# First projection and first feed-forward product of an audio tower: five passes of 128 rows in place of six of 96

## The chip, the core and the metric

The kernel runs on one core of one Trainium2 chip. The metric is device microseconds (us) of one execution, lower is better. Most numbers below are microseconds from the start of the profiled span; the granted clock of TensorE is given as a share of its full speed, 1.00 for 2.4 GHz and 0.50 for 1.2 GHz.

## The reference: what is computed

Eight batches of 750 frames with 192 channels go through three blocks, each ending in 375 tokens of 192 channels. The second and third block are added to a running sum.

```
tok:  depthwise convolution (7 taps) -> pointwise 192x192 -> relu -> max over pairs of frames
      -> real part of a 2-d DFT -> layer norm
attn: n = layernorm(h);  w = n @ w_qkv            (192 -> 768)   <- the first projection
      w is normed over tokens per head; its squares and temp give a softmax over the tokens;
      weighted squares give a gate per head and channel;  -(w * Pi) * gate @ w_out + b_out
ffn:  z = layernorm(h); normed = ln(z); sigmoid scores; the 56 lowest tokens get self-attention,
      the others a mix with a pooled row;  h = z + merged
      n2 = ln(h, g2, b2);  h + gelu(n2 @ W1 + bf1) @ W2 + bf2    <- W1 (192 -> 768): the first
                                                                    feed-forward product
```

## The kernel before

All data of one batch is on the chip: tokens stand either on 125 partitions times three tiles, or, turned, with channels on partitions and the tokens along the free dimension. A software pipeline of three stages runs over the batches: in one step the **front** stage works on batch p (convolution, DFT, first projection, token softmax), the **middle** stage on batch p-1 (routing, keys, attention) and the **last** stage on batch p-2 (feed-forward). Every engine has its own program, written out by hand in `step` (one for each engine), and semaphores join them. So the order on each engine is fixed by the text: an instruction that waits holds up all that stand behind it on that engine. Steps 2 to 7 have all three stages; step 0 has only the front, step 1 no last stage, step 8 no front, step 9 only the last stage.

Products that need more precision than one pass of the type fp32r gives are done in parts. The operand is split into a high part (a ScalarE copy that rounds to fp32r) and a low part (a VectorE subtraction), and high by high, high by low and low by high are summed in PSUM. `split_product` (line 1087) issues these three matmuls, at line 1090. 192 channels are two tiles of 96 partitions (C = 96, CT = 2), so one output tile of 128 channels by 376 tokens takes six matmuls, each with its own weight load: three for each half of the channels.

The two products that the change touches:

- The **first projection**, `qkv(b, j)` on TensorE (line 1138), j = 0 to 5. It comes behind `front_input` (line 1132), six transposes that turn the normed tokens into the PSUM tensor xb; ScalarE copies the high parts (line 892) and VectorE subtracts the low parts (line 468). The result goes to one of two PSUM banks; ScalarE's `squares` copies and squares it (lines 901 and 902), and `qkv(b, j)` waits for the squares of j-2. On ScalarE the squares are interleaved with the middle stage's exponentials (line 977) and with copies of the turned probabilities (line 982). When the last square is done, VectorE makes `rhead` (line 480), for which TensorE's `token_logits` (line 1156) waits.
- The **first feed-forward product**, `forward_up(b, j)` (line 1330), j = 0 to 5, behind `forward_input` (line 1326, also six transposes, into zb). Here one ScalarE copy (line 998) and one VectorE subtraction (line 703) serve both channel halves. The six groups are spread between other work: the first ahead of the middle stage's transposes (`routed_input`), the second ahead of `score_sums` (line 1210), the third and fourth behind the rank sums, the fifth and sixth between small products. ScalarE's `gelus` (line 1004) empty the two banks.

The weights of both are loaded once, with channels on 96 partitions, into a scratch view (`w_qkv32`, laid over the tile probsT), and split there: ScalarE makes the high part (line 869), VectorE the low part (line 408). The W1 load is issued by the sync engine's queue after w_qkv's low part is done.

Of the kernel before, what the change touches and what calls it, by code (L numbers as in the profile page):

```python
# [5 lines left out]
N = S // 2  # L6
P, T = 125, 3
C, CT = 96, 2
H1, IT = 12, 6
# [3 lines left out]
NE = N + 1  # L13
# [21 lines left out]
def audio_tower(nc, dram, out):  # L35
    fp32, bf16, fp32r = mybir.dt.float32, mybir.dt.bfloat16, mybir.dt.float32r
    ALU, ACT, AX = mybir.AluOpType, mybir.ActivationFunctionType, mybir.AxisListType

    with ExitStack() as ctx:
        def sb(name, shape, dt=fp32):  # L40
            return ctx.enter_context(nc.sbuf_tensor(name, shape, dt))

        def signal(name, per_batch=1):
            return Signal(ctx.enter_context(nc.semaphore(name)), per_batch)
# [8 lines left out]
        rows = sb("rows_sb", [P, 8, D])  # L53
        w_qkv = sb("w_qkv_sb", [C, 2, CT, IT * 128], fp32r)
        temp = sb("temp_sb", [128, IT])
# [16 lines left out]
        slot = sb("slot_sb", [Q, 1])  # L72
        w_1 = sb("w_1_sb", [C, 2, CT, IT * 128], fp32r)
        b_1 = sb("b_1_sb", [128, IT])
# [8 lines left out]
        zed = sb("zed", [P, T, D])  # L83
        n2T = sb("n2T", [C, 2, CT, NE], fp32r)

# [8 lines left out]
        xh = even  # L94
        xhT = sb("xhT", [C, 2, CT, NE], fp32r)

# [54 lines left out]
        att = sb("att", [Q, D])  # L151
        w_qkv32 = probsT[0:C].rearrange("c j t q -> c (j t q)")[:, 0:CT * IT * 128].rearrange("c (t i) -> c t i", t=CT)
        w_1_32 = w_qkv32
        n2 = sb("n2", [P, T, D])
# [4 lines left out]

        gelu = sb("gelu", [128, IT, NE])  # L160
        res_f = sb("res_f", [P, T, D])
        y_out = res_f
# [57 lines left out]
        n2t_done, n2_done = signal("n2t_done", T), signal("n2_done", T)  # L220
        n2T_ready, n2T_high, n2T_done = signal("n2T_ready"), signal("n2T_high"), signal("n2T_done")
        w1_ready, gelu_done = signal("w1_ready", IT), signal("gelu_done", IT)
# [4 lines left out]
        def tok(t):  # L227
            return slice(P * t, P * (t + 1))
# [35 lines left out]
        def split_parts(k):  # L264

            weight, parts = ((w_qkv32, w_qkv), (w_1_32, w_1), (w_k32, w_k), (w_v32, w_v), (w_m[:], w_mp))[k]
            return weight, parts[:, 0, :, 0:weight.shape[-1]], parts[:, 1, :, 0:weight.shape[-1]]
# [77 lines left out]
        def _(dve):  # L345
# [110 lines left out]
            def second_norm(b):  # L456
# [3 lines left out]
                for t in range(T):  # L460
                    dve.tensor_scalar(xh[:, t, :], res[:, t, :], ln2[1][:, t, 0:1], ln2[3][:, t:t + 1],
                                      ALU.subtract, ALU.mult).then_inc(xh_done.sem, 1)

            def front_input(b):

                for c in range(CT):
                    dve.wait_ge(*xhT_high.of(b, c + 1))
                    dve.tensor_tensor(xhT[:, 1, c, 0:N], xb[0:C, c, 0:N], xhT[:, 0, c, 0:N], ALU.subtract).then_inc(xhT_done.sem, 1)  # L468

# [230 lines left out]
            def forward_input(b):  # L700

                dve.wait_ge(*n2T_high.of(b))
                dve.tensor_tensor(n2T[:, 1, :, 0:N], zb[0:C, 0:2, 0:N], n2T[:, 0, :, 0:N], ALU.subtract).then_inc(n2T_done.sem, 1)  # L703

# [96 lines left out]
        def _(pool):  # L801
            pool.memset(half3[:], -0.5).then_inc(consts.sem, 1)
            for tokens in (xhT, n2T, nT):
                pool.memset(tokens[:, :, :, N:NE].bitcast(fp32), 0.0).then_inc(pads.sem, 1)
            pool.memset(w_v[:, :, :, D + 1:DV].bitcast(fp32), 0.0).then_inc(pads.sem, 1)
# [52 lines left out]
        def _(act):  # L858
# [26 lines left out]
            def front_input(b):  # L885
                act.wait_ge(*xhT_ready.of(b))
                if first(b):
                    act.wait_ge(pads.sem, PADS)
                else:
                    act.wait_ge(*qkv_ready.before(b))  # L890
                for c in range(CT):
                    act.activation(xhT[:, 0, c, 0:N], xb[0:C, c, 0:N], ACT.Copy).then_inc(xhT_high.sem, 1)
                if first(b):
                    act.wait_ge(consts.sem, FILLS)
# [97 lines left out]
            def forward_input(b):  # L992
                act.wait_ge(*n2T_ready.of(b))
                if first(b):
                    act.wait_ge(pads.sem, PADS)
                else:
                    act.wait_ge(*w1_ready.before(b))
                act.activation(n2T[:, 0, :, 0:N], zb[0:C, 0:2, 0:N], ACT.Copy).then_inc(n2T_high.sem, 1)  # L998

# [76 lines left out]
        def _(pe):  # L1076
            mm = pe.matmul

            def transposes(src, dst):
                for c in range(CT):  # L1080
                    for t in range(T):
                        ins = pe.transpose(dst[0:C, c, tok(t)], src[:, t, chan(c)], ident[0:P, 0:P])  # L1082
                return ins

            pe.wait_ge(first_in.sem, FIRST)

            def split_product(o, a, b, start, stop):

                for k, l in ((0, 0), (0, 1), (1, 0)):
                    ins = mm(o, a[:, k], b[:, l], start=start and k + l == 0, stop=stop and k == 1)  # L1090
                return ins

            def pointwise(b, q):
# [38 lines left out]
            def front_input(b):  # L1132
                if first(b):
                    pe.wait_ge(norm_in.sem, NORM)
                pe.wait_ge(*xh_done.of(b))
                transposes(xh, xb).then_inc(xhT_ready.sem, 1)

            def qkv(b, j):

                if j == 0:  # L1140
                    if first(b):
                        pe.wait_ge(pads.sem, PADS)
                        pe.wait_ge(lows.sem, 1)
                if j >= 2:
                    pe.wait_ge(*sq_done.of(b, j - 1))
                for c in range(CT):
                    if j == 0:
                        pe.wait_ge(*xhT_done.of(b, c + 1))
                    ins = split_product(xb[:, j % 2, 0:NE], w_qkv[:, :, c, 128 * j:128 * j + 128], xhT[:, :, c, :], c == 0, c == 1)
                ins.then_inc(qkv_ready.sem, 1)  # L1150
# [175 lines left out]
            def forward_input(b):  # L1326
                pe.wait_ge(*n2_done.of(b))
                transposes(n2, zb).then_inc(n2T_ready.sem, 1)

            def forward_up(b, j):  # L1330
                if j == 0:
                    pe.wait_ge(*n2T_done.of(b))
                    if first(b):
                        pe.wait_ge(lows.sem, WEIGHTS)
                        pe.wait_ge(*prob_done.of(b))
                    else:
                        pe.wait_ge(*y_done.before(b))
                if j >= 2:
                    pe.wait_ge(*gelu_done.of(b, j - 1))
                for c in range(CT):  # L1340
                    ins = split_product(yb[:, j % 2, 0:NE], w_1[:, :, c, 128 * j:128 * j + 128], n2T[:, :, c, :], c == 0, c == 1)
                ins.then_inc(w1_ready.sem, 1)
# [207 lines left out]
```

## Time and profile before

| what | us |
|---|---|
| runs of the kernel | 609.90, 615.81, 616.28; median 615.81 |
| the profiled execution | 609.72 |
| its span, first to last instruction | 607.8 |
| TensorE matmuls busy | 536.7 (88% of the span) |
| VectorE busy | 427.9 (70%) |
| ScalarE busy | 234.5 (39%) |
| GpSimd busy | 68.5 (11%) |
| mean granted clock of TensorE | 0.927 |

The span is 1.9 us shorter than the profiled execution's own time. That execution is one of the lower ones: it stands 1% under the median. Busy time of TensorE counts each matmul with its run through the array, in which the next one already streams; the pace of a row of matmuls is read from the chain of waits or from the start of one group to the start of the next, not from the mean duration. The busy shares are means over ten steps with different limits.

### The profile page before, as it was taken

To read this page: it belongs to the slowest core of one execution; us is meant where nothing else is said; L and a number is where in the kernel's file an instruction comes from. 1 tells how busy PE (TensorE), PEld (TensorE's weight loads), DVE (VectorE), ACT (ScalarE), POOL (GpSimd) and SP (SyncE) were. 2 spreads that over 40 slices of the span, in tenths; PEclk is the share of its full clock that TensorE was granted. 3 is DMA by queue.
4 is the path that set the end of the run, shared out by engine and by line. 5 is a ranking of instruction groups with operands and counts; after the bars stand their busy time and mean duration, and the time that the engine had idled before them with its cause. 6 is when DMAs were issued, how large, how long until landed. Compare 5 with 4: busy or idle time off the path is not lost.

```text
span 607.8 us, 9498 instructions
## 1 busy us (share of the span) xinstructions
PE 536.7 (88%) x3344; PEld 444.4 (73%) x3344; DVE 427.9 (70%) x1239; ACT 234.5 (39%) x619; POOL 68.5 (11%) x67
## 2 busy tenths in 40 slices
PE   1637498979999999999999999999999999969896
PEld 1426286758877888778887987797778877856586
DVE  6777658675778987798878887887788473843240
ACT  1134113530458135811582257315651457014611
POOL 0010001100030003001210121011200120001000
PEclk9986589676999999999999999999999999967698
DMA  9531000010000100010001000100000000000000
GB/s 215 145 73 38 1 2 1 0 39 1 1 1 5 36 20 1 1 40 19 0 0 38 19 0 0 38 19 0 0 0 20 1 1 1 6 15 1 1 9 30
DMA packets 8217, 12.73 MB, mean 21 GB/s; under 512 B 1896, under 2 KB 6722, under 8 KB 8189
## 3 DMA queue, kind: packets, MB, share of 16 engines
q1 hardware_dynamic: 8189, 12.37, 7.7%
q8 instruction: 16, 0.26, 0.2%
q14 instruction: 12, 0.10, 0.0%
HBM read 10.07 MB, written 2.30 MB: 20 GB/s over the span
## 4 chain that ended last, share of the span: by engine, by line
PE 59%; DVE 16%; ACT 13%; issue 9%; POOL 1%; DMA 1%; ACTq 0%; DVEq 0%; SPq 0%; POOLq 0%
PE xb L1175 9%; PE yb L1090 8%; PE zb L1090 7%; PE xb L1120 5%; ACT w_sq L902 3%; ACT probs L977 3%; PE xb L1129 3%; ACT w_s L901 2%; DVE dw L401 2%; PE xb L1090 2%; DVE w_sq L508 2%; DVE junk L516 2%; PE xb L1156 2%; PE zb L1322 2%; PE yb L1352 2%
## 5 line engine op out<-in xcount | busy, mean ns | idle before, releaser
L815 POOL TENSOR_TENSOR rs<-ve,half 125x3 f32<-125x3 f32 (+1 forms) x32 | 33.4, 1045 | 407.3 <-DVE ve L366 329.6
L383 DVE SCALAR_TENSOR_TENSOR dw<-x_in,w_dw_sb,dw 96x750 f32<-96x750 f32 x84 | 79.0, 990 | 0.2
L1090 PE MATMUL xb<-xhT,w_qkv_sb 96*128 96x376 f32 x288 | 63.6, 366 | 4.8 <-DVE xhT L468 3.4
L1090 PE MATMUL yb<-n2T,w_sb 96*128 96x376 f32 x288 | 60.6, 352 | 4.2 <-DVE n2T L703 3.2
L1090 PEld LDWEIGHTS xb<-xhT,w_qkv_sb 96*128 96x128 f32 x288 | 52.4, 204 | 11.3 <-DVE xhT L468 6.8
L1175 PE MATMUL xb<-scratch,w_sq 128*125 128x192 f32 x288 | 53.0, 347 | 4.1 <-ACT scratch L913 4.1
L1175 PEld LDWEIGHTS xb<-scratch,w_sq 128*125 128x125 f32 x288 | 51.6, 203 | 4.9 <-DVE scratch L530 4.5
L1090 PEld LDWEIGHTS yb<-n2T,w_sb 96*128 96x128 f32 x288 | 49.3, 192 | 6.9 <-DVE n2T L703 4.2
L1352 PE MATMUL yb<-w_sb,gelu 128*125 128x192 f32 x252 | 47.5, 331 | 0.0
L1352 PEld LDWEIGHTS yb<-w_sb,gelu 128*125 128x125 f32 x252 | 40.7, 187 | 2.8 <-issue 2.8
L1120 PE MATMUL xb<-dft_n_sb,pooled_h 125*96 125x376 f32 x96 | 34.2, 510 | 1.0 <-DVE pooled_h L417 0.9
L982 ACT ACTIVATE probsT<-zb 125x384 f32<-125x384 f32 x48 | 26.4, 551 | 21.2 <-PE zb L1286 21.2
L913 ACT ACTIVATE scratch<-w_out_sb,natt 128x192 f32<-128x192 f32 x24 | 9.2, 445 | 64.9 <-DVE natt L528 64.9
L1286 PEld LDWEIGHTS zb<-ident_sb,probs 128*125 128x125 f32 x144 | 23.0, 207 | 13.5 <-issue 10.5
L1004 ACT ACTIVATE gelu<-yb,b_sb 128x375 f32<-128x375 f32 x48 | 26.7, 570 | 14.1 <-PE yb L1090 12.7
L1110 PE MATMUL xb<-w_pw_sb,dw 97*125 97x192 f32 x64 | 17.9, 364 | 14.7 <-DVE dw L401 14.2
L998 ACT ACTIVATE n2T<-zb 96x750 fp32r<-96x750 f32 x8 | 6.3, 792 | 62.1 <-PE zb L1082 62.1
L1286 PE MATMUL zb<-ident_sb,probs 128*125 128x128 f32 x144 | 28.3, 311 | 2.0 <-ACT probs L977 2.0
L508 DVE TENSOR_TENSOR w_sq<-w_s,xb 128x376 f32<-128x376 f32 x48 | 25.2, 538 | 4.8 <-PE xb L1167 4.8
L901 ACT ACTIVATE w_s<-xb 128x375 f32<-128x375 f32 x48 | 25.4, 530 | 6.3 <-PE xb L1090 6.2
L1120 PEld LDWEIGHTS xb<-dft_n_sb,pooled_h 125*96 125x96 f32 x96 | 16.1, 174 | 15.4 <-issue 15.1
L902 ACT ACTIVATE w_sq<-xb 128x375 f32<-128x375 f32 x48 | 25.8, 537 | 0.0
(190 smaller groups left out, 1104.5 us busy)
## 6 DMA issues: line engine op xcount, KB each, us to landing
x_in<-in_x SPq DMA_DIRECT2D x8, 567.0 KB, 4.2
out<-res_f SPq DMA_DIRECT2D x7, 281.2 KB
probsT<-in_w_qkv SPq DMA_DIRECT2D x1, 576.0 KB, 7.5
w_out_sb<-in_w_out SPq DMA_DIRECT2D x1, 576.0 KB
w_sb<-in_w SPq DMA_DIRECT2D x1, 576.0 KB
probsT<-in_w SPq DMA_DIRECT2D x1, 576.0 KB, 4.2
rows_sb<-in_rows SPq DMA_DIRECT2D x1, 504.0 KB
dft_n_sb<-in_dft_n SPq DMA_DIRECT2D x1, 493.5 KB
```

The source lines that it names most:

```text
L383: ins = dve.scalar_tensor_tensor(out=dw[0:C, c, :], in0=src, scalar=w_dw[:, c, k:k + 1], in1=dw[0:C, c, :], op0=ALU.mult, op1=ALU.add)
L508: dve.tensor_tensor(u[:, j, :], w_s[:, j, :], xb[:, j % 2, 0:NE], ALU.mult).then_inc(u_done.sem, 1)
L815: pool.tensor_tensor(out_[:], in_[:], half3[:] if len(in_.shape) == 3 else half3[:, 0, :], ALU.pow).then_inc(rs.sem, 1)
L901: act.activation(w_s[:, j, 0:N], xb[:, j % 2, 0:N], ACT.Copy)
L902: act.activation(w_sq[:, j, 0:N], xb[:, j % 2, 0:N], ACT.Square, accum_out=nrm[:, j:j + 1]).then_inc(sq_done.sem, 1)
L982: act.activation(probsT[:, j, :, :], zb[0:P, 2 + j % 2, 0:T * 128].rearrange("p (t q) -> p t q", q=128), ACT.Copy).then_inc(prT_done.sem, 1)
L1004: act.activation(gelu[:, j, 0:N], yb[:, j % 2, 0:N], ACT.Gelu, bias=b_1[:, j:j + 1]).then_inc(gelu_done.sem, 1)
L1090: ins = mm(o, a[:, k], b[:, l], start=start and k + l == 0, stop=stop and k == 1)
L1120: ins = mm(xb[0:C, c, 0:2 * KF], pooled_h[:, t, chan(c)], dft_n[:, t, :], start=(t == 0), stop=(t == T - 1))
L1175: ins = mm(o, u[:, j, tok(t)], w_oa[:, j, :], start=(j == 0), stop=(j == IT - 1))
L1286: ins = pe.transpose(zb[0:P, 2 + j % 2, 128 * t:128 * t + 128], probs[:, j, tok(t)], ident[:])
L1352: ins = mm(o, gelu[:, j, tok(t)], w_2[:, j, :], start=(j == 0), stop=(j == IT - 1))
```

## The change

The 192 channels are cut 128 + 64 in place of 96 + 96. The tokens' tile gets three slots of 128 partitions: slot 0 is the high part of channels 0 to 127, slot 2 their low part, and slot 1 holds both parts of channels 128 to 191, the low part on partitions 0 to 63 and the high part on partitions 64 to 127. The weights get four slots: 0 and 2 are the high and low part of channels 0 to 127, 1 and 3 those of channels 128 to 191, each written twice, once above the other. So five matmuls with 128 rows give the sum, and it holds low by low for the last 64 channels besides. The transposes take 128 columns each, the second one channels 64 to 191, so that channels 128 to 191 come out on partitions 64 to 127.

The feed-forward tokens are now split by two ScalarE copies and two VectorE subtractions, one pair for each slot, where one of each served before. The two weight loads carry 128 partitions (the last 64 channels twice: 768 KB each in place of 576 KB), and their scratch view lies over the tile gelu in place of probsT. The pad memsets follow the new shape.

```diff
-        w_qkv = sb("w_qkv_sb", [C, 2, CT, IT * 128], fp32r)
+        w_qkv = sb("w_qkv_sb", [128, 4, IT * 128], fp32r)
-        n2T = sb("n2T", [C, 2, CT, NE], fp32r)
+        n2T = sb("n2T", [128, 3, NE], fp32r)
-        xhT = sb("xhT", [C, 2, CT, NE], fp32r)
+        xhT = sb("xhT", [128, 3, NE], fp32r)
...
+        w_qkv32 = gelu[:].rearrange("c j n -> c (j n)")[:, 0:2 * IT * 128].rearrange("c (t i) -> c t i", t=2)
+        w_1_32 = w_qkv32
...  VectorE
+            def stacked_low(c, parts, bank):
+                if c == 0:
+                    return dve.tensor_tensor(parts[:, 2, 0:N], bank[:, 0, 0:N], parts[:, 0, 0:N], ALU.subtract)
+                return dve.tensor_tensor(parts[0:64, 1, 0:N], bank[64:128, 1, 0:N], parts[64:128, 1, 0:N], ALU.subtract)
             def front_input(b):
                 for c in range(CT):
                     dve.wait_ge(*xhT_high.of(b, c + 1))
-                    dve.tensor_tensor(xhT[:, 1, c, 0:N], xb[0:C, c, 0:N], xhT[:, 0, c, 0:N], ALU.subtract).then_inc(xhT_done.sem, 1)
+                    stacked_low(c, xhT, xb).then_inc(xhT_done.sem, 1)
             def forward_input(b):
-                dve.wait_ge(*n2T_high.of(b))
-                dve.tensor_tensor(n2T[:, 1, :, 0:N], zb[0:C, 0:2, 0:N], n2T[:, 0, :, 0:N], ALU.subtract).then_inc(n2T_done.sem, 1)
+                for c in range(CT):
+                    dve.wait_ge(*n2T_high.of(b, c + 1))
+                    stacked_low(c, n2T, zb).then_inc(n2T_done.sem, 1)
...  ScalarE
-                    act.activation(xhT[:, 0, c, 0:N], xb[0:C, c, 0:N], ACT.Copy).then_inc(xhT_high.sem, 1)
+                    act.activation(xhT[64 * c:128, c, 0:N], xb[64 * c:128, c, 0:N], ACT.Copy).then_inc(xhT_high.sem, 1)
-                act.activation(n2T[:, 0, :, 0:N], zb[0:C, 0:2, 0:N], ACT.Copy).then_inc(n2T_high.sem, 1)
+                for c in range(CT):
+                    act.activation(n2T[64 * c:128, c, 0:N], zb[64 * c:128, c, 0:N], ACT.Copy).then_inc(n2T_high.sem, 1)
...  TensorE
+            def stacked_transposes(src, dst):
+                for c in range(CT):
+                    for t in range(T):
+                        ins = pe.transpose(dst[0:128, c, tok(t)], src[:, t, 64 * c:64 * c + 128], ident[0:P, 0:P])
+                return ins
+            def stacked_product(o, w, j, x, rest=None):
+                cols = slice(128 * j, 128 * j + 128)
+                mm(o, w[:, 0, cols], x[:, 0, :], start=True, stop=False)
+                mm(o, w[:, 2, cols], x[:, 0, :], start=False, stop=False)
+                if rest is not None:
+                    pe.wait_ge(*rest)
+                mm(o, w[:, 0, cols], x[:, 2, :], start=False, stop=False)
+                mm(o, w[:, 1, cols], x[:, 1, :], start=False, stop=False)
+                return mm(o, w[:, 3, cols], x[:, 1, :], start=False, stop=True)
             def qkv(b, j):
-                for c in range(CT):
-                    if j == 0:
-                        pe.wait_ge(*xhT_done.of(b, c + 1))
-                    ins = split_product(xb[:, j % 2, 0:NE], w_qkv[:, :, c, 128 * j:128 * j + 128], xhT[:, :, c, :], c == 0, c == 1)
+                if j == 0:
+                    pe.wait_ge(*xhT_done.of(b, 1))
+                ins = stacked_product(xb[:, j % 2, 0:NE], w_qkv, j, xhT, xhT_done.of(b) if j == 0 else None)
             def forward_up(b, j):
-                for c in range(CT):
-                    ins = split_product(yb[:, j % 2, 0:NE], w_1[:, :, c, 128 * j:128 * j + 128], n2T[:, :, c, :], c == 0, c == 1)
+                ins = stacked_product(yb[:, j % 2, 0:NE], w_1, j, n2T)
...  host: the weights' layout
+    def stacked(w):
+        return np.stack([w[0:128], np.concatenate([w[128:], w[128:]])], 1)
```

## Rows read from the trace of the kernel before

**Rows 1.** Stretch, us, busy of PE, PEld, DVE, ACT, POOL; clock, DMA share, GB/s:
```profile
282.93:346.35 63.42, 61.81 (x419) 51.86 (x419) 52.07 (x151) 28.65 (x77) 8.41 (x7) 1.00 0.05 14
```

**Rows 2.** Chain of waits in that step: start, us, what ended last:
```profile
282.93 1.02 PE yb L1090 x6
283.95 0.64 PE zb L1082 x6
...
293.41 0.33 PE zb L1210 x3
...
307.14 0.79 PE xb L1082 x6
...
308.03 0.49 ACT xhT L892
...
320.05 0.47 ACT w_sq L902 x2
```

**Rows 3.** A stretch inside the first projection, columns as in rows 1:
```profile
316.00:318.00 2.00, 2.00 (x15) 2.00 (x14) 2.00 (x4) 2.00 (x9) 0.00 (x0) 1.00 0.00 0
```

**Rows 4.** TensorE in order of time: start, us, instructions, idle before, releaser:
```profile
309.14 2.33 PE L1090 MATMUL xb<-xhT,w_qkv_sb 96*128 96x376 f32 x12 [0.39 <-DVE xhT L468]
...
321.39 1.45 PE L1156 MATMUL xb<-w_sq,rhead 128*32 128x375 f32 x12 [0.60 <-DVE rhead L480]
...
326.38 0.61 PE L1167 MATMUL xb<-pi_parts,head_sel_sb 128*128 128x376 f32 x2 [0.27 <-DVE pi_parts L501]
```

**Rows 5.** One line's matmuls: ns minimum/median/maximum, 128 rows and 96:
```profile
L1167 PE MATMUL xb<-pi_parts,head_sel_sb x48: 332/437/682, 64.8 to 521.2; 128*128 128x376 f32 x48
...
L1090 PE MATMUL xb<-xhT,w_qkv_sb x288: 328/334/682, 48.5 to 508.5; 96*128 96x376 f32 x144
```

**Rows 6.** VectorE, and one group of weight loads (PEld), in order of time:
```profile
281.11 0.93 DVE L703 TENSOR_TENSOR n2T<-zb,n2T 96x750 fp32r<-96x750 f32 x1
281.96 1.07 DVE L557 SCALAR_TENSOR_TENSOR nr<-nr,rs,rows_sb 125x192 f32<-125x192 f32 x3
...
292.82 0.18 DVE L590 RECIPROCAL nr<-sexp 125x3 f32<-125x3 f32 x1
293.09 0.46 PEld L1210 LDWEIGHTS zb<-ident_sb,nr 125*125 125x125 f32 x3
...
305.13 0.96 DVE L461 TENSOR_SCALAR even<-res,ag,rs 125x192 f32<-125x192 f32 x3 [0.38 <-POOL rs L815]
...
308.54 1.00 DVE L468 TENSOR_TENSOR xhT<-xb,xhT 96x375 fp32r<-96x375 f32 x2 [1.68 <-ACT xhT L892]
```

**Rows 7.** TensorE in order of time, steps 0 and 1:
```profile
48.49 9.71 PE L1090 MATMUL xb<-xhT,w_qkv_sb 96*128 96x376 f32 x36 [1.24 <-DVE xhT L468]
...
112.68 4.08 PE L1090 MATMUL xb<-xhT,w_qkv_sb 96*128 96x376 f32 x12
...
126.02 1.97 PE L1156 MATMUL xb<-w_sq,rhead 128*32 128x375 f32 x12 [2.45 <-DVE rhead L480]
```

**Rows 8.** TensorE in order of time, steps 8 and 9:
```profile
535.85 1.80 PE L1090 MATMUL yb<-n2T,w_sb 96*128 96x376 f32 x6 [3.17 <-DVE n2T L703]
...
590.38 3.35 PE L1090 MATMUL yb<-n2T,w_sb 96*128 96x376 f32 x18 [0.54 <-DVE res_f L711]
```

**Rows 9.** Stretches of steps 0 and 1, columns as in rows 1:
```profile
50.00:55.00 5.00, 5.00 (x18) 5.00 (x17) 5.00 (x8) 2.39 (x8) 0.00 (x0) 0.50 0.01 3
...
125.00:130.00 5.00, 3.98 (x33) 2.13 (x36) 3.54 (x8) 1.56 (x6) 0.00 (x0) 0.68 0.21 64
```

**Rows 10.** ScalarE in order of time, start-up:
```profile
25.57 1.47 ACT L869 ACTIVATE w_qkv_sb<-probsT 96x1536 fp32r<-96x1536 f32 x1
...
47.29 0.85 ACT L892 ACTIVATE xhT<-xb 96x375 fp32r<-96x375 f32 x2 [8.30 <-PE xb L1082]
```

**Rows 11.** DMA issues: size, microseconds from issue to landing:
```profile
probsT<-in_w_qkv SPq DMA_DIRECT2D x1, 576.0 KB, 7.5
...
probsT<-in_w SPq DMA_DIRECT2D x1, 576.0 KB, 4.2
```

More of the change, by code:

```diff
@@ L72, in audio_tower @@
         slot = sb("slot_sb", [Q, 1])
-        w_1 = sb("w_1_sb", [C, 2, CT, IT * 128], fp32r)
+        w_1 = sb("w_1_sb", [128, 4, IT * 128], fp32r)
         b_1 = sb("b_1_sb", [128, IT])
@@ L151, in audio_tower @@
         att = sb("att", [Q, D])
-        w_qkv32 = probsT[0:C].rearrange("c j t q -> c (j t q)")[:, 0:CT * IT * 128].rearrange("c (t i) -> c t i", t=CT)
-        w_1_32 = w_qkv32
         n2 = sb("n2", [P, T, D])
@@ L220, in audio_tower @@
         n2t_done, n2_done = signal("n2t_done", T), signal("n2_done", T)
-        n2T_ready, n2T_high, n2T_done = signal("n2T_ready"), signal("n2T_high"), signal("n2T_done")
+        n2T_ready, n2T_high, n2T_done = signal("n2T_ready"), signal("n2T_high", CT), signal("n2T_done", CT)
         w1_ready, gelu_done = signal("w1_ready", IT), signal("gelu_done", IT)
@@ L264, in split_parts @@
         def split_parts(k):
-            weight, parts = ((w_qkv32, w_qkv), (w_1_32, w_1), (w_k32, w_k), (w_v32, w_v), (w_m[:], w_mp))[k]
+            if k < 2:
+                parts = (w_qkv, w_1)[k]
+                return w_qkv32, parts[:, 0:2, :], parts[:, 2:4, :]
+            weight, parts = ((w_k32, w_k), (w_v32, w_v), (w_m[:], w_mp))[k - 2]
             return weight, parts[:, 0, :, 0:weight.shape[-1]], parts[:, 1, :, 0:weight.shape[-1]]
@@ L802, in _ @@
             pool.memset(half3[:], -0.5).then_inc(consts.sem, 1)
-            for tokens in (xhT, n2T, nT):
-                pool.memset(tokens[:, :, :, N:NE].bitcast(fp32), 0.0).then_inc(pads.sem, 1)
+            for tokens in (xhT, n2T):
+                pool.memset(tokens[:, :, N:NE].bitcast(fp32), 0.0).then_inc(pads.sem, 1)
+            pool.memset(nT[:, :, :, N:NE].bitcast(fp32), 0.0).then_inc(pads.sem, 1)
             pool.memset(w_v[:, :, :, D + 1:DV].bitcast(fp32), 0.0).then_inc(pads.sem, 1)
@@ L1135, in front_input @@
                 pe.wait_ge(*xh_done.of(b))
-                transposes(xh, xb).then_inc(xhT_ready.sem, 1)
+                stacked_transposes(xh, xb).then_inc(xhT_ready.sem, 1)
             def qkv(b, j):
@@ L1327, in forward_input @@
                 pe.wait_ge(*n2_done.of(b))
-                transposes(n2, zb).then_inc(n2T_ready.sem, 1)
+                stacked_transposes(n2, zb).then_inc(n2T_ready.sem, 1)
             def forward_up(b, j):
@@ L1514 @@
         "ident": np.eye(128, dtype=f),
-        "w_qkv": tiles(a["L0_attn_w_qkv"], C),
+        "w_qkv": stacked(a["L0_attn_w_qkv"]),
         "temp": a["L0_attn_temp"][:, 0][head],
@@ L1533 @@
         "slot": np.where(q < SEL, q, -1).astype(f)[:, None],
-        "w_1": tiles(a["L0_ffn_W1"], C),
+        "w_1": stacked(a["L0_ffn_W1"]),
         "b_1": a["L0_ffn_bf1"].reshape(IT, 128).T,
```

## The prediction

> **What bounds the kernel now.** I read the table of stretches first. A full step lasts 63.42 us, TensorE is busy in 61.81 of it at a granted clock of 1.00 [rows 1]; steps 2 to 7 are all of this kind. That is only a first hint, since a busy matmul includes its run through the array. So I read the chain of waits inside one such step [rows 2]. It has two parts. From 282.93 to 307.93 it goes through TensorE alone, from group to group, and the six groups of the feed-forward product lie in it. From 308.03 to 320.5 it goes through ScalarE, which is busy without a gap (2.00 of 2.00 us, [rows 3]) with exponentials, squares and copies; the six groups of the first projection lie beside it. Then VectorE makes rhead, and TensorE, which has been idle for 0.60 us, starts the token logits at 321.39 [rows 4]. The rest of the step is softmax, spread and the long output product, which the change does not touch. So the two halves of the change must be priced apart: one shortens TensorE where it ends last, the other where ScalarE does.
>
> **A pass.** In the chain six passes take 1.02 us [rows 2], so one costs 0.17 us at full clock, though a single matmul lasts at least 328 ns [rows 5]: they overlap. The trace has no row of consecutive passes with 128 rows and 376 columns. The nearest is the spread, which has that shape: its shortest matmul lasts 332 ns against 328 for 96 rows [rows 5]. Bounds for what a pass with 128 rows costs more: nothing, and 0.03 us, a fifth, at which five would cost as much as six. I take nothing, as the two minima differ by 1%.
>
> A rule of the Trainium skill speaks about this overlap (TensorE: Matmul & The Clock Gate, Part 3): a weight load runs beside matmuls in flight only if it goes to another row group. By it each pass would pay load and matmul in turn, the removed pass would be worth about twice as much, and the full steps would gain some 10 us more. The trace disagrees: 0.17 us a pass leaves no room for it.
>
> **Transposes.** Twelve per full step get weight loads of 128 columns in place of 96. Six with 96 columns take 0.64 us in the chain, 0.107 each; three with 125 columns take 0.33 us, 0.110 each [rows 2]. So 12 x 0.003 = 0.04 us per step at most; I take zero. The skill has a price for this that speaks against the change (same page, LDWEIGHTS): a load costs its columns divided by 1.2 in ns. By that 32 more columns are 27 ns, an estimate of 0.3 us per step if nothing hid it, and the sum would be 2 to 3 us worse. The rows show that it is hidden.
>
> **Full steps, feed-forward product.** Six passes go, 6 x 0.17 = 1.02 us. What is late next, group by group:
> - First group: behind it the transposes need nr, done at 281.96 + 1.07 = 283.03, and run from 283.95 in the chain [rows 2, 6]. The split of the feed-forward tokens into two pieces puts a second instruction on VectorE just ahead of nr: two such halves of the projection's tokens cost 1.00 us together against 0.93 for the one [rows 6], so nr comes 0.07 us later. That leaves over 0.5 us of slack, and the 0.17 us is won. The second ScalarE copy is off the chain.
> - Second group: score_sums waits for the reciprocal that ends at 292.82 + 0.18 = 293.00, and its weight load starts at 293.09 [rows 6]. Here only about 0.05 us is won, the rest becomes a wait.
> - The other four groups: full, 0.68 us. The next thing that could be late is the transposes of the projection's input, which need xh at 305.13 + 0.96 = 306.09 [rows 6] and start at 307.14 [rows 2]; 1.05 us of slack, and xh itself, which hangs on score_sums by way of VectorE and GpSimd, moves 0.22 us forward with it.
>
> Sum 0.17 + 0.05 + 0.68 = 0.90 us per step, six steps: **5.4 us**. Bounds: 0 and 6.1 us.
>
> **Full steps, first projection.** Six more passes go, but ScalarE has no gap to give up. The first group cannot end sooner, as its last three passes still wait for the second low part, and before, too, three passes followed that wait. So zero; TensorE only comes to the token logits earlier and waits there, about 0.5 us longer on top of 0.60 [rows 4], the rest spread in front of the later groups. It is hidden by ScalarE; if that cover were gone it would be worth up to 1 us per step.
>
> **Steps 0 and 1.** In step 0 there are no exponentials on ScalarE, and TensorE is granted 0.50 until about 55 us [rows 9]. 36 passes take 9.71 us [rows 7], 0.27 each, so six fewer are 1.6 us at most; once the clock is back ScalarE's copy and square come close, so I take 0.95. In step 1 the first two groups take 4.08 us for 12 passes [rows 7], 0.34 each; two passes less are 0.68 before ScalarE rules again; I take 0.6.
>
> **Steps 8 and 9.** In step 8 six passes take 1.80 us when the clock is down [rows 8], 0.30 each: two groups at that price and four at 0.17 are 1.3 us, less 0.1 for the extra split instruction, which lies in the open there: 1.2. In step 9 the first three groups take 3.35 us for 18 passes [rows 8], and gelu and the second product alternate with them; six passes at 0.17 are 1.0. The entry of step 9 waits for the result of the batch before, not for the split, so nothing is lost there.
>
> **Start-up.** Both weight loads grow by a third. At their own time to landing, 7.5 and 4.2 us [rows 11], that is at most 2.5 and 1.4 us. The copy of w_qkv runs at 25.57, long after its load, which is issued within the first 10 us; after the copy of W1 ScalarE idles 8.30 us until the transposes [rows 10]. So zero; without that cover 1.4 us once. The splits themselves cost by their free size, which stays at 1536.
>
> **The sum.** 5.4 + 0.95 + 0.6 + 1.2 + 1.0 = 9.15, say 9.2 us. The profiled execution took 609.72 us (span 607.8 and 1.9 around it): 600.6. Two of the three runs shown lie near 616, and the median of 615.81 is 6 us above the profiled execution; the passes go in either kind of run, so from the median it is 606.6. I predict 606 us.
>
> **Rivals.**
> 1. *The next waits eat half.* If score_sums, the reciprocal or xh are later than the rows suggest, or a pass with 128 rows costs 0.015 us more, the full steps give 2 to 3 us in place of 5.4, and the whole about 6: 610 us from the median. For it: the second group has only 0.09 us of slack. Against: the others have 0.5 or more. Chance 0.15.
> 2. *The clock falls for a short time in each full step.* In step 1 TensorE idled 2.45 us ahead of the token logits [rows 7], and the stretch from 125 to 130 us shows a clock of 0.68 after 1.00 before [rows 9]: 64% of 5 us, 3.2 us, at 1.2 GHz. In full steps the idle there is 0.60 us with the clock at 1.00; the change makes it about 1.1 us and adds small waits before. If the clock fell each time, 3.2 us at half rate would lose 1.6 us of TensorE's work, less the 0.27 us that it waits for the softmax anyway [rows 4]: 1.3 x 6 = 8 us, and 614 us in all, no change. Against: 1.1 us is less than half of the idle time at which it fell. Chance 0.11.
> 3. *Slower: the clock stays down.* Same place, but at 1.2 GHz through the spread and the output product, where TensorE is again dense. To decide against the change it must last long: a stretch T of half clock costs T/2 - 0.27 us, and 0.9 us of gain per step is gone at T = 2.3 us; 1% slower needs about 2.55 us per step more, T = 7.5 us. With 12 us it would be 5.7 us in each of six steps, +34 - 9 = +25, 641 us. Against: in step 1 the first fall was over within 3.2 us. Chance 0.07.
> 4. *ScalarE is not the cover.* If the projection's passes count as well, another 4 to 6 us: 601 us from the median. Against it is ScalarE's gapless stretch [rows 3]. Chance 0.05.
>
> That the change does not do what it says I hold excluded: one of six issued matmuls is gone in each group by the text. The forecast itself gets 0.62.
>
> **The numbers.** The forecast is 600.6 to 606.6, with the kind of run deciding; rival 4 pulls the lower end to 598, rivals 1 and 2 the upper end to 614; beyond lies rival 3 and half of rival 2. About 1%, 6 us, is what a measurement of this kernel can tell from no change. Faster by over 1%: forecast and rival 4, 0.67. Within 1%: rivals 1 and 2, 0.26. Slower: 0.07.
>
> **What would show it.** Right: full steps of about 62.5 us; five-pass groups of 0.85 us in the chain; a wait in front of score_sums of about 0.1 us; an idle time of about 1.1 us ahead of the token logits, and ScalarE still without a gap from the table load to the last square; transposes at 0.11 us. Wrong: passes with 128 rows at 0.20 us; a granted clock under 1.00 in the full steps; ScalarE waiting for the projection; the first projection starting late at 48 us because of the larger loads.

## The result, and the profile of the changed kernel

The changed kernel took 596.53 us (median of four runs, 595.51 to 599.11) against 614.83 for the kernel before on the same chip: a ratio of 0.9722, with a 95% interval of 0.9658 to 0.9787. In two more sets of runs the ratio was 0.9775 (0.9684 to 0.9866) and 0.9802 (0.9746 to 0.9858). The forecast was 606 us with a low end of 598: the direction was right, and the gain was about twice the forecast's 9.2 us in the first set, and 14.2 and 10.6 us in the others.

The mean granted clock differs from one execution of the same kernel to the next, from 0.906 (621.4 us) to 0.930 (609.0 us) in 56 runs of the kernel before on four chips, and the time follows it.

The stretches between two starts of the output product show where the profiled execution (596.45 us, span 594.7) is shorter than that of before. Columns as in [rows 1]; the five stretches are the start-up with step 0, step 1, step 2, five full steps, and the end with steps 8 and 9. The kernel before:
```profile
0.00:73.25 73.25, 34.17 (x121) 25.02 (x121) 52.31 (x131) 16.59 (x39) 4.40 (x14) 0.83 0.38 98
73.25:143.52 70.27, 62.87 (x341) 49.90 (x341) 47.23 (x132) 22.19 (x66) 6.04 (x5) 0.79 0.03 9
143.52:208.86 65.34, 63.87 (x420) 53.77 (x420) 51.92 (x151) 28.64 (x77) 8.43 (x7) 0.97 0.04 10
208.86:526.02 317.16, 309.26 (x2091) 259.35 (x2091) 248.20 (x737) 143.20 (x385) 42.06 (x35) 1.00 0.04 10
526.02:607.80 81.78, 66.52 (x378) 56.40 (x376) 28.29 (x91) 23.91 (x52) 7.59 (x6) 0.81 0.04 11
```
The changed kernel:
```profile
0.00:71.26 71.26, 32.11 (x114) 23.38 (x115) 52.50 (x131) 16.73 (x39) 4.41 (x14) 0.83 0.37 106
71.26:137.57 66.31, 56.96 (x334) 44.97 (x335) 47.09 (x133) 22.25 (x66) 6.04 (x5) 0.86 0.03 9
137.57:202.76 65.19, 63.46 (x406) 52.29 (x407) 52.09 (x151) 28.95 (x78) 8.40 (x7) 0.96 0.04 10
202.76:516.64 313.88, 304.95 (x2033) 249.30 (x2032) 250.30 (x742) 144.78 (x390) 42.04 (x35) 1.00 0.04 11
516.64:594.70 78.06, 61.59 (x365) 51.90 (x364) 28.69 (x93) 24.27 (x54) 7.54 (x6) 0.86 0.04 12
```
Five full steps give 317.16 - 313.88 = 3.28, that is 0.66 us each, less than the forecast 0.90. The two ends give 1.99, 3.96 and 3.72, in all 9.7 us, where the forecast had 3.75; step 1 and the end have a higher granted clock than before (0.86 for 0.79, and 0.86 for 0.81).

Inside a full step, first TensorE in order of time (start, us, instructions, idle before): the five passes of the first feed-forward group, the first pass of the projection, and the token logits.
```profile
275.92 0.47 PE L1116 MATMUL yb<-n2T,w_sb 128*128 128x376 f32 x1
276.23 0.33 PE L1117 MATMUL yb<-n2T,w_sb 128*128 128x376 f32 x1
276.39 0.33 PE L1120 MATMUL yb<-n2T,w_sb 128*128 128x376 f32 x1
276.56 0.33 PE L1121 MATMUL yb<-n2T,w_sb 128*128 128x376 f32 x1
276.73 0.33 PE L1122 MATMUL yb<-n2T,w_sb 128*128 128x376 f32 x1
...
301.67 0.44 PE L1116 MATMUL xb<-xhT,w_qkv_sb 128*128 128x376 f32 x1 [0.40 <-DVE xhT L470]
...
314.06 1.45 PE L1186 MATMUL xb<-w_sq,rhead 128*32 128x375 f32 x12 [0.67 <-DVE rhead L489]
```
The passes start 0.17 us apart, as those of 96 rows did [rows 2], and the shortest still takes 328 ns [rows 5]. Then the chain of waits of the same step, where [rows 2] had its counterpart; "issue" is time in which the engine waited for nothing that the profile shows:
```profile
277.07 0.64 PE zb L1094 x6
277.71 3.93 PE xb L1151 x12
...
286.52 0.39 PE zb L1240 x3
...
299.64 0.80 PE xb L1101 x6
300.55 0.49 ACT xhT L903
301.06 0.55 DVE xhT L470
301.88 0.34 issue
302.23 0.35 DVE w_mp L580
302.61 0.56 DVE nmax L653
```
Transposes with 128 columns cost 0.80 us beside 0.79 with 96 in [rows 2]; score_sums has become 0.06 us longer. Two places were not in the forecast. The transform of the pooled tokens (L1151) takes 3.93 us in the chain, where the kernel before has
```profile
284.59 3.79 PE xb L1120 x12
...
309.57 0.35 DVE w_mp L571
...
309.96 0.56 DVE nmax L644
```
and between xhT and the exponentials the chain runs over VectorE, through w_mp to the attention's maximum nmax. The last two lines show that it did so before the change, too; the forecast had read the chain there only up to ScalarE's copy of xhT.

### The profile page after: what moved, and what is told of

Its sections match the earlier page's. It is cut to its first block, busy times and chain, and to the rows that moved or that the text cites. A ratio compares the mean times of both kernels' runs of the same rounds, so it can differ in the third digit from the quotient of the medians.

```text
span 594.7 us, 9326 instructions
## 1 busy us (share of the span) xinstructions
PE 519.1 (87%) x3248; PEld 421.8 (71%) x3248; DVE 430.7 (72%) x1247; ACT 237.0 (40%) x627; POOL 68.4 (12%) x67
## 4 chain that ended last, share of the span: by engine, by line
PE 57%; DVE 18%; ACT 13%; issue 9%; POOL 1%; DMA 1%; DVEq 0%; ACTq 0%; SPq 0%; POOLq 0%
PE xb L1205 9%; PE zb L1109 7%; PE xb L1151 6%; ACT probs L988 3%; PE xb L1160 3%; ACT w_sq L913 3%; DVE w_sq L517 3%; ACT w_s L912 2%; DVE junk L525 2%; DVE dw L404 2%; PE xb L1186 2%; PE yb L1116 2%; PE yb L1381 2%; PE xb L1141 2%; PE xb L1142 2%
## 5 line engine op out<-in xcount | busy, mean ns | idle before, releaser
L1151 PE MATMUL xb<-dft_n_sb,pooled_h 125*96 125x376 f32 x96 | 34.0, 506 | 1.0 <-DVE pooled_h L420 0.9
L1010 ACT ACTIVATE n2T<-zb 128x375 fp32r<-128x375 f32 (+1 forms) x16 | 7.7, 481 | 62.8 <-PE zb L1101 62.6
L1151 PEld LDWEIGHTS xb<-dft_n_sb,pooled_h 125*96 125x96 f32 x96 | 15.7, 171 | 15.7 <-issue 14.6
L1116 PE MATMUL xb<-xhT,w_qkv_sb 128*128 128x376 f32 x48 | 21.1, 439 | 5.6 <-DVE xhT L470 3.5
L525 DVE CUSTOM_DVE_ANT_0 junk<-w_sq,w_s 128x375 f32<-128x375 f32 x48 | 25.4, 540 | 0.0
L1197 PE MATMUL xb<-pi_parts,head_sel_sb 128*128 128x376 f32 x48 | 18.3, 433 | 7.8 <-DVE pi_parts L510 6.5
L1116 PE MATMUL yb<-n2T,w_sb 128*128 128x376 f32 x48 | 20.2, 422 | 4.3 <-DVE n2T L471 3.4
```

What stands on the lines that cost most here:

```text
L525: dve.tensor_tensor_reduce(out=junk[:, j % 2, 0:N], in0=u[:, j, 0:N], in1=w_s[:, j, 0:N], scale=1.0, scalar=0.0, op0=ALU.mult, op1=ALU.add ...
L1116: mm(o, w[:, 0, cols], x[:, 0, :], start=True, stop=False)
L1151: ins = mm(xb[0:C, c, 0:2 * KF], pooled_h[:, t, chan(c)], dft_n[:, t, :], start=(t == 0), stop=(t == T - 1))
```

## The experiments

The questions: is it the missing pass or the height of the passes that makes the ends shorter, and what takes a third of the forecast gain in the full steps? The table has each kernel's median with its ratio to the kernel before on its own chip, the median granted clock of its runs, the time at 1.2 GHz worked out from it run by run as 2 x (1 - clock) x span (the median), and a full step, the mean of the five between starts of the output product in the profile.

| kernel | passes x rows | us | ratio (95%) | clock | us at 1.2 GHz | full step |
|---|---|---|---|---|---|---|
| before (56 runs) | 6 x 96 | 614.81 | | 0.918 | 100.5 | 63.43 |
| changed (16 runs) | 5 x 128 | 599.58 | 0.972 to 0.980 | 0.933 | 80.1 | 62.78 |
| five96 | 5 x 96 | 602.31 | 0.9787 (0.9735, 0.9838) | 0.921 | 95.5 | 62.51 |
| six128 | 6 x 128 | 608.47 | 0.9856 (0.9805, 0.9907) | 0.935 | 78.8 | 63.62 |
| pad128 | 6 x 128, 32 of them zero | 610.35 | 0.9927 (0.9884, 0.997) | 0.937 | 76.7 | 63.43 |
| only_ffn | 5 x 128, 6 x 96 | 602.90 | 0.9756 (0.9705, 0.9806) | 0.927 | 87.8 | 62.63 |
| only_qkv | 6 x 96, 5 x 128 | 610.42 | 0.9938 (0.9897, 0.998) | 0.924 | 92.6 | 63.56 |
| all_rows | 5 x 128 | 597.54 | 0.9729 (0.9662, 0.9797) | 0.937 | 74.4 | 62.78 |
| max_first | 5 x 128 | 602.34 | 0.9815 (0.9737, 0.9892) | 0.926 | 89.5 | 62.63 |
| max_rows (12 runs) | 5 x 128 | 598.10 | 0.9733 and 0.9773 | 0.932 | 81.0 | 62.44 |

In the rows with two counts the feed-forward product stands first. One run of six128 took 1742.57 us; it is left out of the clock columns. The kernel before differs by chip: it spent 102.2 us at 1.2 GHz (median) beside five96, six128, only_ffn and only_qkv, 103.2 beside pad128 and all_rows, and 88.8 beside max_rows and max_first.

**five96**, the kernel before with one pass taken out of each group. It leaves out the product of the weights' low part with the tokens' high part for channels 96 to 191, in both products.
```diff
-  ins = split_product(o, a, b, c == 0, c == 1)
+  if c == 0:
+      return split_product(o, a, b, True, False)
+  mm(o, a[:, 0], b[:, 0], start=False, stop=False)
+  return mm(o, a[:, 0], b[:, 1], start=False, stop=True)
```


> The kernel before with one of its six passes left out in both products (weight low by token high of channels 96 to 191; that part of the sum is missing). Five passes of 96 rows, one split instruction as before. Theory 'passes': as fast as the changed kernel or 1 to 4 us faster, since VectorE's longer split is not paid: 13 to 21 us below the kernel before, full steps 62.4 to 62.6 us. Rival 'rows': only what the forecast counted, 8 to 10 us below the kernel before, and the clock at either end as in the kernel before.

602.31 us, and full steps of 62.51, 0.92 us below the kernel before: the forecast's 0.90 for the passes holds. The clock changed little (0.911 to 0.925 over its runs), as "rows" has it. The time does not fit "rows": 615.86 on the same chip less 602.31 is 13.55 us, inside the 13 to 21 of "passes" and above the 8 to 10 of "rows". So the missing pass is worth more than the forecast had, without any height; the next part compares the kernels at an equal clock.

**six128**, the changed kernel with a sixth pass in each group, the product of the two low parts for channels 0 to 127.
```diff
   mm(o, w[:, 2, cols], x[:, 0, :], start=False, stop=False)
+  mm(o, w[:, 2, cols], x[:, 2, :], start=False, stop=False)
```


> The new layout with a sixth pass put back: low by low of channels 0 to 127, so six passes of 128 rows where the kernel before has six of 96. Theory 'passes': the gain comes from the count alone, so it is gone and the two split instructions remain as cost: full steps 63.4 to 63.8 us, time 0 to +4 us against the kernel before, within 1%. Rival 'rows': passes of 128 rows keep TensorE's granted clock up, or bring it back sooner, in the steps at either end; then the excess over the forecast (some 8 of 17 us) stays: 6 to 9 us faster than before, with clearly less time at 1.2 GHz.

608.47 us. The full steps are 0.19 us longer than before the change, and yet the kernel is 1.4% faster, since its clock was 0.933 to 0.941, above all 17 runs of the kernel before on the same chip (0.906 to 0.930). Where the clock comes back differs between executions: in the profiled one (608.84 us) the start, step 1 and step 2 are shorter than before, and the end is not:
```profile
523.19:607.00 83.81, 67.34 (x378) 57.93 (x376) 28.69 (x93) 24.29 (x54) 7.55 (x6) 0.82 0.04 11
```

**only_ffn** and **only_qkv**, the change in one product alone; the other has its tiles, split, transposes and six passes as before.
```diff
-  xhT = sb("xhT", [128, 3, NE], fp32r)
+  xhT = sb("xhT", [C, 2, CT, NE], fp32r)              # only_ffn; n2T likewise in only_qkv
```


> Only the feed-forward product in five passes of 128 rows; the first projection as before. Theory 'passes': full steps keep the gain but for the 0.16 us that the projection's split costs, 62.6 us each; steps 8 and 9 gain some 3 us; steps 0 and 1 unchanged: 7 to 9 us faster than before. Rival 'rows': the same in the full steps, and step 1's clock as before, so also some 8 us; this run tells where the gain lies rather than why.

> Only the first projection in five passes of 128 rows; the feed-forward product as before. Forecast of record: full steps gain nothing here, steps 0 and 1 1.6 us. Theory 'passes': full steps 63.4 to 63.6 us, steps 0 and 1 together 1.5 to 3 us shorter: 0 to 3 us faster than before, within 1%. Rival 'rows': steps 0 and 1 together 5 to 7 us shorter because the clock is up for longer: 5 to 8 us faster. Rival 'cover': ScalarE is not the bound there and full steps lose 0.5 us or more each: 4 to 6 us faster.

The feed-forward half gives 0.80 us per full step and the projection's half costs 0.13; together 0.67, and the whole change measures 0.66. So the projection's passes are hidden, as forecast, but its new split is not. In time both gain more than "passes" gave them: only_ffn 13.0 us from the 615.86 before (7 to 9 were expected), only_qkv 5.4 (0 to 3).

**pad128** keeps the kernel before and its six passes, and only makes the four tiles 128 rows high, with zeros in rows 96 to 127.
```diff
-  xhT = sb("xhT", [C, 2, CT, NE], fp32r)              # and w_qkv, n2T, w_1
+  xhT = sb("xhT", [128, 2, CT, NE], fp32r)
+  for tile in (xhT, w_qkv, n2T, w_1,):
+      pool.memset(tile[C:128].bitcast(fp32), 0.0).then_inc(pads.sem, 1)
```


> The kernel before, with the tiles of both operands of the projection and of the first feed-forward product made 128 rows high and rows 96 to 127 set to zero: twelve passes of 128 rows a step at the same column count, the splits and the transposes as before, and 32 rows of each pass that add nothing. Theory 'rows' (the passes' height alone brings TensorE back to 2.4 GHz earlier in the steps at either end; it went from some 102 us at 1.2 GHz with 96 rows to some 79 us with six passes of 128): the same 75 to 85 us at half clock, full steps of 63.4 as before, 607 to 610 us, ratio 0.985 to 0.992. Rival 'data' (it is rows that carry values that do so, zeros do not count): half-clock time stays at 95 to 105 us, 614 to 616 us, ratio 0.997 to 1.003. Rival 'split' (the gain at the ends comes from the new splits and transposes, which begin the product in another order): 614 to 616 us as well, but with the clock of before in every stretch.

610.35 us against 616.98, a little more than "rows" gave it (607 to 610, ratio 0.985 to 0.992); the 76.7 us at 1.2 GHz are inside its 75 to 85. Its runs had a granted clock of 0.930 to 0.941, those of the kernel before on that chip 0.906 to 0.930. Its stretches, which answer to the five of the kernel before above:
```profile
0.00:75.10 75.10, 32.88 (x121) 24.23 (x121) 55.49 (x131) 16.71 (x39) 12.20 (x18) 0.85 0.37 96
75.10:145.37 70.27, 62.72 (x340) 49.65 (x340) 47.28 (x132) 22.22 (x66) 6.04 (x5) 0.79 0.03 9
145.37:210.54 65.17, 63.69 (x420) 53.59 (x420) 51.91 (x151) 28.69 (x77) 8.41 (x7) 0.97 0.04 10
210.54:527.69 317.15, 309.12 (x2092) 259.19 (x2092) 248.14 (x737) 143.44 (x385) 42.03 (x35) 1.00 0.04 10
527.69:606.00 78.31, 62.30 (x377) 53.19 (x376) 28.27 (x91) 23.95 (x52) 7.61 (x6) 0.89 0.04 12
```
The five full steps are the same to 0.01 us, and in this execution so is step 1, at 0.79 as before. The end has the same matmuls with the same columns, a clock of 0.89 for 0.81, and is 3.47 us shorter. The start is 1.85 us longer beside GpSimd's 12.20 us of work for 4.40, which holds the added zero fills (that they cause it is not tested). So the height of the passes alone can bring the clock back, zeros included, and the rivals "data" and "split" fall.

**all_rows**: ScalarE copies all 128 rows in both pieces of a split; rows 0 to 63 of the shared part are then written again by VectorE.
```diff
-  act.activation(xhT[64 * c:128, c, 0:N], xb[64 * c:128, c, 0:N], ACT.Copy)
+  act.activation(xhT[:, c, 0:N], xb[:, c, 0:N], ACT.Copy)          # n2T likewise
```


> The changed kernel, with ScalarE's two copies in each stacked split made over all 128 rows, so that no instruction of ScalarE changes its rows from its neighbour's; rows 0 to 63 of the shared part are written by ScalarE and then again by VectorE, as the order of waits has it already. Theory 'range' (two neighbouring instructions overlap only where their rows are the same: two copies of xhT took 0.85 us with 96 rows each and 0.99 with 128 and 64): the pair returns to 0.84 to 0.88 us, and as ScalarE sets the projection's end, each full step shortens by 0.12 to 0.16 us, to some 62.63; in all 595 to 596 us beside 596.5. Rival 'shape' (the pair is longer as the copies are higher or write another place): 0.96 to 1.0 us and full steps of 62.75 to 62.80, no gain.

The copies overlap again, 0.86 us for the two, and the full step stays at 62.78 all the same. ScalarE in order of time in the changed kernel:
```profile
300.55 0.99 ACT L903 ACTIVATE xhT<-xb 128x375 fp32r<-128x375 f32 x2 [0.55 <-PE xb L1101]
...
303.19 0.57 ACT L988 ACTIVATE probs<-zb,nmax 128x375 f32<-128x375 f32 x1
```
and in this one, then a line of its waits in that step (who waited for whom: us in total, times, longest):
```profile
300.99 0.86 ACT L903 ACTIVATE xhT<-xb 128x375 fp32r<-128x375 f32 x2 [0.55 <-PE xb L1101]
```
```profile
ACT probs L988 <- DVE nmax L653: 0.3, 1, 0.3
```
"range" was right about the pair and wrong about the step: ScalarE now waits 0.3 us for VectorE's nmax, ahead of which stand the lows of xhT and w_mp. That gave the next theory, two paths of about equal length into the first exponential.

**max_rows** and **max_first**: w_mp goes on VectorE behind the second maximum, with all_rows' copies and without.
```diff
-  if middle:
-      pooled_row(q)
   for j in range(IT):
       if middle:
           attention_max(q, j)
+          if j == 1:
+              pooled_row(q)
```


> The kernel with ScalarE's copies over all rows, and on VectorE w_mp (0.35 us, first read some 19 us later by a product of TensorE) moved from ahead of the attention's first maximum nmax to behind its second. Theory 'two paths' (ahead of the projection's first exponential, ScalarE waits for nmax, and nmax stands on VectorE behind the two lows of xhT and w_mp; the changed split made both ScalarE's path and VectorE's path 0.14 us longer, so that mending ScalarE's alone gave nothing): here both are short, the idle time of ScalarE ahead of its first probs goes from 0.3 to under 0.1 us, and each full step shortens by 0.2 to 0.3 us, to 62.48 to 62.58; in all 593.5 to 595.5 us in the better runs. Rival 'other end' (the lows of xhT themselves, through TensorE's projection, or the pooled tokens set the step, not nmax): full steps stay at 62.75 to 62.80.

> The changed kernel with that move of w_mp alone, ScalarE's copies as the change has them (0.99 us for two). Theory 'two paths': ScalarE's own path (two copies, the load of its table, a hint) is now the later one; full steps shorten by 0.08 to 0.15 us, to 62.63 to 62.70, half of what both edits give. Rival 'VectorE alone' (ScalarE's copies never counted): the same 62.48 to 62.58 as with both edits. Rival 'other end': 62.75 to 62.80.

The full steps are 62.44 us (62.48 to 62.58 were expected) and 62.63 (62.63 to 62.70), as "two paths" has it, and both rivals fall. The medians, 597.14 and 602.34 us, hang on the clock at the ends, as the table shows. max_first also has five passes of 128 rows, and yet its 89.5 us at 1.2 GHz (83.6 to 105.6, six runs) lie in the range of the kernel before on its chip, 88.8 (85.0 to 109.7). ScalarE of max_rows in order of time shows the wait gone:
```profile
302.99 0.86 ACT L903 ACTIVATE xhT<-xb 128x375 fp32r<-128x375 f32 x2 [0.55 <-PE xb L1101]
303.87 1.28 ACT L1063 ACT_TABLE_LOAD   x1
305.16 0.20 ACT L1063 ACTIVATE table_hint<-ones 1x1 f32<-1x1 f32 x1
305.27 0.55 ACT L988 ACTIVATE probs<-zb,nmax 128x375 f32<-128x375 f32 x1
```
From the copies to the exponential it takes 305.27 - 302.99 = 2.28 us, where the changed kernel takes 303.19 - 300.55 = 2.64; max_first and the kernel before both take 2.51 (305.36 - 302.85 and 310.54 - 308.03). Six full steps at 62.78 - 62.44 = 0.34 us would be 2.0 us in all. Side by side on one chip, as two runs of their own:

> The kernel with all rows copied and w_mp moved, beside the changed kernel on one chip, to see whether it beats both. Full steps of 62.45 to 62.47 us as in the run before. Theory 'two paths' with the ends as they fall: 1.5 to 2.5 us under the changed kernel's run with the same granted clock, some 594 to 595 us at a clock of 0.941 and some 598 at 0.930.

> The changed kernel as it is, beside it: full steps of 62.75 to 62.80 us, some 596.6 us at a granted clock of 0.941 and 599 to 603 at 0.924 to 0.933.

598.13 us (595.96 to 600.04) against 600.43 (597.66 to 601.03), with full steps of 62.45 and 62.76. The 2.3 us are about what the steps promise, but the runs overlap; that it beats the changed kernel is shown for the steps and likely for the whole. The changed kernel beside all_rows was run as

> The changed kernel as it is, on the same chip as the others of this set. All theories: 595 to 599 us, full steps of 62.75 to 62.80 us, 70 to 76 us at half clock; it is the base for the small difference of the kernel with all rows copied.

It took 602.79 us (596.73 to 608.53), more than expected, with clocks of 0.916 to 0.941; its full steps were 62.78. A difference of 5 us from all_rows, whose steps are the same, lies in the clock at the ends (101.9 us at 1.2 GHz in its longest run, 70.2 in its shortest).

## Why the prediction was too small

**The clock at the ends, the step that failed.** "A pass: I take nothing" was right for the full steps and was carried to the ends, where passes were priced at the clock that the trace of before had there [rows 7, 8, 9]. The clock entered the prediction only as something that could fall (rivals 2 and 3); that it could come back was no case at all. Over the runs of the kernel before, each microsecond more at 1.2 GHz goes with 0.36 us more of its time: a straight line through its 56 runs gives 578.9 + 0.36 t, with t the time at 1.2 GHz. The same line through 16 runs of the changed kernel is 570.9 + 0.36 t, with the same slope. So at an equal clock the change is worth 578.9 - 570.9 = 8.0 us, close to the forecast 9.2, and over all chips the other 0.36 x (100.5 - 80.1) = 7.3 us go with the clock. Side by side on one chip it is less: t falls from 103.2 to 91.3 and from 88.7 to 80.3, worth 4.3 and 3.0 us. In the set that was forecast it is more: the changed kernel has t from 70.2 to 80.0, the clocks of the kernel before are not on record there, and by its line 614.83 us stand for t = 99.8; of the 18.3 us some 10 are then the clock.

That the height of the passes can do this is shown by pad128, which changes nothing else of the passes, and by six128: their t (71.5 to 85.7 and 71.3 to 81.3) lies below almost every run of the kernel before on their chips (85.0 to 116.5). The line holds for six128: 607.3 us at its 78.8, and 6 x 0.19 = 1.1 for its full steps, are 608.4, and 608.11 was measured (the median of its five runs with a clock below 1.00). For pad128 it gives 606.5 and 1.85 for the start, 608.4 where 610.35 was measured; 2 us stay open. Height is not all that decides: max_first's six runs gain nothing clear at the clock, and the changed kernel's own six runs beside pad128 reach from 70.2 to 101.9. What else does stays open.

That 8.0 lies near 9.2 is in part luck. By the same line five96, five passes without the new splits, is worth some 11 us at an equal clock: 5.5 in its full steps and over 5 at the ends, where the forecast had 3.75. (Its profile shows 3.3 at the ends, 1.5 up to the end of step 2 and 1.8 behind the full steps, but with 93.6 us at 1.2 GHz for 88.7.) The new splits then take 1.6 us back in the full steps and, as the difference that is left, some 1.4 at the ends, for which the forecast had 0.1. At an equal clock only_ffn is worth 7.6 us and only_qkv 1.8, as "passes" expected of them.

The Trainium skill (TensorE: Matmul & The Clock Gate, Part 1, "What's actually happening") says that the gate follows how busy TensorE has lately been. The runs agree that it is what TensorE does that moves the clock; they add that matmuls of the same number and columns, but of more rows, can move it too.

**The new splits, a term of the full step that was mis-sized.** "nr comes 0.07 us later ... and the 0.17 us is won" failed, and so did the price of nothing for the split of xhT. The prediction sized both by two halves that start at the same row [rows 6]. The stacked pieces start at different rows. VectorE of the changed kernel in order of time, first a piece from row 0, then one from row 64, then nr from row 0:
```profile
274.40 0.54 DVE L470 TENSOR_TENSOR n2T<-zb,n2T 128x375 fp32r<-128x375 f32 x1
274.97 0.55 DVE L471 TENSOR_TENSOR n2T<-zb,n2T 64x375 fp32r<-64x375 f32 x1
275.55 1.08 DVE L566 SCALAR_TENSOR_TENSOR nr<-nr,rs,rows_sb 125x192 f32<-125x192 f32 x3
276.66 0.62 DVE L420 SCALAR_TENSOR_TENSOR pooled_h<-xb,even 125x192 f32<-125x192 f32 x2
```
None starts before the other has ended: from the first low to nr it is 1.15 us. In [rows 6] nr starts 0.85 us after the one low, which is 0.93 us long. So nr is 0.30 us later in place of 0.07. The pooled tokens behind it were, in the kernel before, at
```profile
282.94 0.61 DVE L417 SCALAR_TENSOR_TENSOR pooled_h<-xb,even 125x192 f32<-125x192 f32 x2
```
which is 1.83 us behind the low at 281.11; now it is 2.26. The slack in front of the transposes holds, and the 0.17 us is won there, but the transform that reads the pooled tokens loses 0.14 of it again (3.93 for 3.79). It takes 3.79 in five96 (old split) and in six128 (new split, but the transposes start a pass later), and 3.92 in only_ffn, which has the new split and five passes. The Trainium skill (VectorE: DVE Perf Modes, "Two Vector instructions with no wait between them") has this as a rule: an instruction whose input or output starts in another group of 32 rows than the last one did in that memory is held until all earlier ones are done. The trace agrees on VectorE, by the rows just shown; the prediction should have used it. No run here changes the rows of a piece on VectorE alone.

The split of xhT costs 0.13 us by only_qkv, and the 2.64 us for 2.51 show where: on VectorE the lows end later and push w_mp and nmax, on ScalarE the two copies take 0.99 for 0.85 us. 0.92 for the passes, less 0.14 and 0.13, is 0.65; 0.66 was measured.

**ScalarE as the cover: right with a gap.** The projection's passes are hidden (only_qkv: no gain, so rival 4 falls), and ScalarE is busy throughout their middle, as in [rows 3]:
```profile
310.00:312.00 2.00, 2.00 (x13) 1.73 (x12) 1.85 (x3) 2.00 (x9) 0.00 (x0) 1.00 0.00 0
```
But the argument went from that stretch to the whole path from 308.03 on, whose first 2.5 us belong to VectorE as much as to ScalarE.

**Right by their sizes:** passes of 128 rows at 0.17 us; transposes; a wait of 0.06 us in front of score_sums; the clock at 1.00 in all full steps, so rivals 2 and 3 fall. Rival 1 had the direction of the full steps, 6 x 0.66 = 4.0 us between its 2 to 3 and the forecast's 5.4, but by the new splits and not by the waits that it named. **Wrong by its size, without weight:** the idle time ahead of the token logits went from 0.60 to 0.67 us, not to 1.1. Two sums do not come out: in rival 3 the 2.55 us per step already hold the 0.9, so T is 2 x (2.55 + 0.27) = 5.6 us and not 7.5; and a pass worth twice as much would give 6 x 1.02 = 6.1 us more in the full steps, not some 10.

## What to carry to other kernels

Where a kernel spends part of its time at 1.2 GHz, a change in what TensorE does there has two prices, one at an equal clock and one through the clock; read how the time of a kernel follows the granted clock over its own runs, and ask in both directions. Fuller passes can be worth it for the clock alone (pad128, with zeros: ratio 0.9927), but the clock also differs between runs of one kernel, so compare them on one chip and over many runs. Before a tile is split by rows, count which instructions of its engine change their first row, and price each as one that starts only when its neighbour is done; and where a stretch is said to be bound by one engine, check what that engine waits for at the stretch's entry, not only in its middle.

## What the runs showed of the hardware

- Six passes with 32 rows of zeros moved the clock like six with 128 rows of data: 76.7 us at 1.2 GHz with zeros (pad128) and 78.8 with data (six128), where 96 rows had 103.2 and 102.2 on the same chips.
- Two neighbouring ScalarE copies of 375 columns took 0.85 us when both were 96 rows high, 0.86 when both were 128, and 0.99 when the second started at row 64. One alone takes 0.47 to 0.48 us.
- Matmuls of 128 rows and 376 columns follow one another by 0.17 us at the full clock and 0.31 at 1.2 GHz, with weight loads of 128 columns between them.
